# A second shared PSUM bank, and the side work laid out anew, in a windowed-attention and expert-mixing block

## The chip, the cores and the metric

The kernel runs on one core of one Trainium2 chip. The metric is the device time in microseconds of one execution.

## What is computed

The input is `x`, 16 images of 56 x 56 positions with 32 channels. Two residual blocks follow each other:

```
x = x + attention(norm(x))     # windows of 7x7 rolled by 3, 4 heads of 8 channels, mask and relative bias after the softmax
t = t + experts(norm(t))       # router over 8 experts, softmax, best 2, their outputs mixed by renormalised probability
```

In the attention the softmax comes first, and bias and mask are added to its result; so the product of bias and mask with the values is a term of its own (`ob`). The normalisations take mean and variance over the 32 channels of a position. Everything is float32 at the borders.

## The kernel before

The work is cut into 16 units (`UNITS`) of 16 x 49 positions each, a half of two images. A unit passes through these steps; `w` in a name below means an older unit, `v` a younger one.

- **Norm 1**: `load` (SP, 12 DMAs, L504), then `norm1_center` (DVE sum L852, POOL subtraction L546), `norm1_square` (ACT L683), `norm1_scale` (DVE sum L858, POOL `pow` L557 and multiplication L561). `keep` (POOL, L569) copies the input with the bias of the projection into `x_kept`, which the residual L915 of the unit two earlier reads.
- **Pre work**: `xt` 0, 1 (transposes L1128), `qk` 0 to 3 (products L1136), `place` (POOL L603) and `kmask` (ACT L723) which lay queries and keys out by head, `v` 0, 1 (L1147), `ob` 0, 1 (L1163).
- **Attention** in four groups `g`: `maximum` (PE L1181, then on DVE the reduction L874 and the two small steps L888 and L890 that write `ms`), `shift` (PE transposes L1189, ACT copy L768 to `mr`), `scores` (PE L1204 and L1210, ACT exponential L777), `pv` (PE L1225, DVE L897 and L901, POOL L611).
- **After it**: `ot` 0, 1 (PE L1236, ACT L756), `y` 0, 1 (PE L1246) with the residual `back` 0, 1 (DVE L915), norm 2 (`norm2_center`: DVE L864 and POOL L579; `norm2_square`: ACT L692; `norm2_scale`: DVE L870, POOL `pow` L590 and multiplication L594), `x2t` 0, 1 (PE L1261, ACT L786), `router` (PE L1269, DVE L922), `replicate` (7 DMAs on SP), `top2` 0 to 4 on DVE, 5 to 7 on POOL (L628 to L644), `top2_exp` (ACT).
- **Mixing**: `wt` (PE L1282, ACT L794), `mix` 0 to 16 (PE L1293 into `ps_weight`, DVE multiplication L989; at 5, 9, 13 and 16 also products L1310 into the sum in `ps_acc`, at 5 and 13 begun by L1305), `mix_drain` 0, 1 (ACT L801), `final` 0, 1 (PE L1253, DVE L998), `store` (12 DMAs).

**Order.** All engines walk one list (`program`). After a head written out in `PROLOGUE`, a `macro_step` takes one unit (`att`) through its four groups and puts side tasks between the fixed steps:

```python
for g in range(GROUPS):
    yield "scores", att, g
    yield from side((g, 0))
    ...  # "maximum" of the next group
    yield from side((g, 1))
    yield "pv", att, g
    yield from side((g, 2))
    ...  # "shift" of the next group
    yield from side((g, 3))
```

`SIDE_TASKS[(g, place)]` is written out by hand. A task is done for another unit than `att`: pre work for the next one, norm 1 for the one after that, `y` to `top2` for the one before, and `wt`, `mix` and `final` for the one before that. Each engine takes the steps of this list that are its own, strictly in order, and waits on semaphores. After the last macro step, `TAIL` names in which order the three chains that are left run: chain 0 is the mixing of unit 14, chain 1 is `ot` 1 to `top2` of unit 15, chain 2 the mixing of unit 15. Before the `wt` of unit 15, `keep_awake` issues 24 matmuls (L1093).

**Banks.** PSUM has four banks `ps_win` for the windows, `ps_pv`, `ps_weight` for the mixing's weights, `ps_acc` for its sum, and `ps_shared`, through which all 17 other fills of a unit pass one after the other (10 of the pre work, 2 `ot`, 2 `y`, 2 `x2t`, 1 `router`). `shared_free` lets PE wait, before each fill, until the fill before it in `SHARED_ORDER` has been drained.

Of the kernel before, what the change touches and what calls it, by code (L numbers as in the profile page):

```python
# [37 lines left out]
N = WS * WS  # L38
E = 8
# [30 lines left out]
PRE_ORDER = ("keep", "xt", "qk", "place", "kmask", "v", "ob")  # L70
LATE = ("wt", "mix", "mix_drain", "final", "store")
SIDE_TASKS = {
    (0, 0): [("ot", 1), ("keep", 0), ("wt", 0), ("y", 0), ("mix", 0), ("back", 0), ("mix", 1), ("y", 1), ("back", 1), ("norm2_center", 0)],
    (0, 1): [("xt", 0), ("mix", 2)],
    (0, 2): [],
    (0, 3): [("mix", 3), ("norm2_square", 0), ("xt", 1), ("mix", 4), ("norm2_scale", 0)],
    (1, 0): [("qk", 0), ("load", 0), ("mix", 5)],
    (1, 1): [("qk", 1), ("mix", 6)],
    (1, 2): [],
    (1, 3): [("mix", 7), ("qk", 2)],  # L80
    (2, 0): [("mix", 8), ("x2t", 0), ("norm1_center", 0), ("mix", 9)],
    (2, 1): [("x2t", 1), ("mix_drain", 0)],
    (2, 2): [("replicate", 0), ("kmask", 0), ("mix", 10), ("router", 0), ("mix", 11), ("qk", 3), ("place", 0), ("mix", 12), ("place", 1)],
# [5 lines left out]
}  # L89
# [10 lines left out]

TAIL = ((1, 1), (0, 1), (1, 6), (0, 1), (1, 1), (0, 11), (1, 2), (0, 1), (1, 1), (0, 1), (1, 1), (0, 1), (1, 3), (0, 1), (1, 1), (0, 2), (1, 2), (0, 4), (2, 2), (1, 1), (2, 5), (1, 1), (2, 5), (1, 1), (2, 12))


def later(name, i):

    return 1 if name in PRE_ORDER else 0 if (name, i) == ("ot", 0) else -1

# [169 lines left out]
def metaformer_block(nc, x, weights, rel_table, consts, consts_bf16, out):  # L279
    with ExitStack() as ctx:  # L280
# [192 lines left out]

        rel_list = list(rel_loads())

        def pre_bank(v, fill):

            return ps_weight if v.number == 0 and fill % 2 else ps_shared

        def weight_bank(w, fill):  # L480

# [6 lines left out]

        def token_bank(w, fill):

            spare = w.number == UNITS - 1 and fill in (1, 3)
            return ps_win[:, 3, :] if spare else ps_shared

        block = ctx.enter_context(nc.Block())

# [178 lines left out]
        def _(act):  # L674
# [172 lines left out]
        def _(dve):  # L847
# [72 lines left out]
            def router(w, _):  # L920
                dve.wait_ge(token_filled, upto("token_filled", w, 4))
                nc.vector.tensor_tensor(  # L922
                    logits[:, :, :], ps_shared[0:ROWS, 0:TOK * E].rearrange("p (t e) -> p t e", e=E),
                    rb[:, :].unsqueeze(1).to_broadcast([ROWS, TOK, E]), ALU.add).then_inc(token_drained, 1)

            at = [0]
# [160 lines left out]
        def _(pe):  # L1087
# [7 lines left out]
            def shared_free(name, u, i):  # L1095

                at = SHARED_ORDER.index((name, i))
                for back in range(1, 2 * len(SHARED_ORDER)):
                    lap, k = divmod(at - back, len(SHARED_ORDER))
                    before, j = SHARED_ORDER[k]  # L1100
                    w = u.moved(lap - later(name, i) + later(before, j))
                    if w is not None:
                        kind, first = SHARED_BANK[before]
                        drained = {"pre": pre_drained, "ot": ot_drained, "token": token_drained}[kind]
                        pe.wait_ge(drained, upto(f"{kind}_drained", w, first + j))
                        return

            def token_free(name, w, i):

                if token_bank(w, (0 if name == "y" else 2) + i) is ps_shared:  # L1110
                    shared_free(name, w, i)
                else:
                    pe.wait_ge(probs_ready, upto("probs_ready", w))

            def pre_free(v, i, fill):

# [170 lines left out]
            def mix(w, i):  # L1287
# [90 lines left out]
```

## Time and profile before

| what | value |
|---|---|
| median of 3 runs | 817.04 us (816.79 to 819.18) |
| the profiled execution | 821.02 us, its span 819.2 us |
| PE busy | 677.5 us, 83% of the span |
| DVE, POOL, ACT busy | 544.2, 516.6, 387.3 us |
| mean granted TensorE clock | 0.940 |

The span is the time from the first to the last instruction. The granted clock is 1.0 at 2.4 GHz and 0.5 at 1.2 GHz; a value between is a mean over a stretch with both.

### The profile page before, as it was taken

How to read it: one execution, taken by the hardware profiler on the slowest of the kernel's cores; microseconds unless marked ns; L12 is line 12 of the kernel's file. 1: busy time of each engine (PE TensorE's matmuls, PEld its weight loads, DVE VectorE, ACT ScalarE, POOL GpSimd, SP SyncE). 2: the span in 40 equal slices, each digit the busy share in tenths (PEclk: the TensorE clock that was granted, in tenths of full speed). 3: DMA queues.
4: the chain of work that ended last, by engine and by line, in shares of the span. 5: the costliest groups of instructions: out<-in, count | busy, mean ns of one | idle time of the engine just before them, and what ended most of it. 6: DMA issues, size and time to landing. Idle time of an engine off the chain costs nothing.

```text
span 819.2 us, 29441 instructions
## 1 busy us (share of the span) xinstructions
PE 677.5 (83%) x12632; PEld 443.1 (54%) x12632; DVE 544.2 (66%) x1003; ACT 387.3 (47%) x641; POOL 516.6 (63%) x555
## 2 busy tenths in 40 slices
PE   0777877979798989989798989989897989878675
PEld 0455554656556655645656565656556556645331
DVE  7352557867676767758676767768686667676544
ACT  1645462646464564636454554646464455612100
POOL 4736677586867768584868767685857666551520
PEclk9999898999999999979999999999998999987777
DMA  2000030313122130413131130413131030403040
GB/s 71 20 22 3 25 77 22 81 42 81 32 62 51 38 85 23 91 32 80 33 70 42 42 82 22 97 26 81 42 82 41 22 81 10 93 2 80 20 99 20
DMA packets 16961, 41.48 MB, mean 51 GB/s; under 512 B 9280, under 2 KB 9408, under 8 KB 15296
## 3 DMA queue, kind: packets, MB, share of 16 engines
q1 hardware_dynamic: 16240, 38.59, 21.2%
q8 instruction: 100, 1.64, 0.8%
q10 hardware_dynamic: 592, 1.01, 0.4%
q14 instruction: 29, 0.24, 0.1%
HBM read 7.47 MB, written 6.42 MB: 17 GB/s over the span
## 4 chain that ended last, share of the span: by engine, by line
PE 56%; DVE 23%; issue 11%; ACT 5%; POOL 4%; ACTq 0%; DVEq 0%; POOLq 0%
DVE mx L874 8%; PE ps_win L1210 7%; PE ps_acc L1310 6%; PE ps_shared L1136 6%; PE ps_weight L1293 5%; PE ps_win L1181 5%; PE ps_pv L1225 5%; PE ps_shared L1163 5%; PE ps_shared L1246 4%; DVE zt L989 4%; PE ps_shared L1147 3%; PE ps_win L1204 3%; DVE x L915 2%; DVE ms L888 2%; PE ps_acc L1305 2%
## 5 line engine op out<-in xcount | busy, mean ns | idle before, releaser
L874 DVE TENSOR_REDUCE mx<-ps_win 128x32 f32<-128x1568 f32 x64 | 114.5, 1789 | 66.5 <-PE ps_win L1181 65.9
L989 DVE TENSOR_TENSOR zt<-ps_weight,x 128x392 f32<-128x392 f32 x118 | 66.2, 561 | 83.0 <-PE ps_weight L1293 82.4
L1225 PEld LDWEIGHTS ps_pv<-vb,pt 128*49 128x49 f32 x4096 | 103.4, 127 | 14.5 <-issue 12.1
L777 ACT ACTIVATE pt<-ps_win 128x1568 f32<-128x1568 f32 x64 | 94.6, 1478 | 33.0 <-PE ps_win L1210 32.5
L611 POOL TENSOR_TENSOR on<-on,obs 128x256 f32<-128x256 f32 x64 | 46.6, 728 | 98.2 <-DVE on L901 72.6
L1225 PE MATMUL ps_pv<-vb,pt 128*49 128x18 f32 x4096 | 108.3, 200 | 0.0
L1293 PE MATMUL ps_weight<-wt,const_bf_tile 96*128 96x392 bf16 x234 | 82.3, 352 | 28.0 <-DVE zt L989 19.5
L989 DVE TENSOR_TENSOR x<-ps_weight,x 128x392 f32<-128x392 f32 x116 | 65.5, 564 | 33.3 <-PE ps_weight L1293 32.3
L768 ACT COPY mr<-ps_win 128x512 bf16<-128x512 bf16 x64 | 37.4, 584 | 87.7 <-PE ps_win L1189 87.7
L590 POOL TENSOR_TENSOR st<-st,minus_half 112x28 f32<-112x28 f32 x16 | 77.0, 4812 | 1.3
L557 POOL TENSOR_TENSOR st<-st,minus_half 112x28 f32<-112x28 f32 x16 | 76.9, 4809 | 1.3
L603 POOL TENSOR_SCALAR qbd<-qp,const_tile 128x392 f32<-128x392 f32 x128 | 76.2, 608 | 0.0
L1210 PE MATMUL ps_win<-qbd,kp 32*49 32x196 f32 x2048 | 74.7, 351 | 0.0
L723 ACT ACTIVATE kbd<-kp,const_tile 128x392 f32<-128x392 f32 x128 | 69.4, 621 | 0.0
L1181 PE MATMUL ps_win<-kbd,qp 32*49 32x196 f32 x2048 | 60.3, 344 | 6.0 <-ACT pt L777 5.1
L1136 PE MATMUL ps_shared<-xt,weight_tile 128*128 128x392 f32 x124 | 60.8, 574 | 2.1 <-ACT xt L701 0.6
L1293 PEld LDWEIGHTS ps_weight<-wt,const_bf_tile 96*128 96x128 bf16 x234 | 23.0, 98 | 71.0 <-DVE zt L989 40.6
L701 ACT COPY xt<-ps_shared 128x448 f32<-128x448 f32 (+1 forms) x31 | 15.8, 511 | 85.2 <-PE ps_shared L1128 85.2
L1181 PEld LDWEIGHTS ps_win<-kbd,qp 32*49 32x49 f32 x2048 | 35.3, 122 | 33.7 <-ACT pt L777 19.7
L1246 PE MATMUL ps_shared<-weight_tile,ot 128*112 128x128 f32 x218 | 32.7, 291 | 21.7 <-ACT ot L756 17.3
L716 ACT ACTIVATE kp<-ps_shared,weight_tile 128x392 f32<-128x392 f32 x30 | 17.6, 588 | 59.8 <-PE ps_shared L1136 59.8
L1163 PE MATMUL ps_shared<-vb,bt 128*64 128x256 f32 (+3 forms) x564 | 39.6, 280 | 6.7 <-ACT ot L756 3.0
(141 smaller groups left out, 1369.1 us busy)
## 6 DMA issues: line engine op xcount, KB each, us to landing
x<-x SPq DMA_DIRECT2D x48, 392.0 KB, 5.1
x<-x2t SPq DMA_DIRECT2D x64, 98.0 KB, 2.2
xin<-x SPq DMA_DIRECT2D x32, 150.0 KB
out<-xo SPq DMA_DIRECT2D x32, 150.0 KB
xin<-x SPq DMA_DIRECT2D x32, 18.0 KB
out<-xo SPq DMA_DIRECT2D x30, 18.0 KB
xin<-x SPq DMA_DIRECT2D x32, 15.6 KB
xin<-x SPq DMA_DIRECT2D x32, 1.9 KB
```

The lines of the kernel that those rows point to most:

```text
L557: nc.gpsimd.tensor_tensor(st1[:, 4, :], st1[:, 3, :], minus_half[:, :], ALU.pow).then_inc(rstd1, 1)
L590: nc.gpsimd.tensor_tensor(st2[:, 4, :], st2[:, 3, :], minus_half[:, :], ALU.pow).then_inc(rstd2, 1)
L603: nc.gpsimd.tensor_scalar(qbd[i][:, :, h, :], qp[v.par][:, 8 * i:8 * i + 8, :], head_rows[:, h:h + 1], 1.0, ALU.mult, ALU.mult).then_inc(q ...
L777: nc.scalar.activation(pt[g % 2].rearrange("p a x h n -> p a (x h n)"), ps_win[:, :, 0:2 * HN], ACT.Exp).then_inc(probs_ready, 1)
L874: nc.vector.tensor_reduce(mx[g % 2].rearrange("n a x h -> n a (x h)"), ps_win[:, :, 0:8 * N].rearrange("n a (k m) -> n a k m", m=N), AX, A ...
L989: nc.vector.tensor_tensor(tokens if eh else zt[:, a, :], weight_bank(w, 1 + i)[:, 0:HALF], tokens, ALU.mult).then_inc(weight_drained, 1)
L1136: mm(pre_bank(v, 2 + i)[:, 0:HALF], (wk if i % 2 else wq)[:, :], xt[:, 8 * b:8 * b + 8, :, :].rearrange("p q k i -> p (q k i)"), start=Tru ...
L1163: ins = mm(bank[PAD * x:PAD * x + PAD, groups, a0:a1, k, :], bt[:, h, last_row + column, :], values[:, x, groups, a0:a1, h, 0:2 * D], star ...
L1181: ins = mm(ps_win[PAD * k:PAD * k + N, a, HN * x:HN * x + HN], qp[u.par][r, q, :], kbd[g // 2][r, q % 8, :, :].rearrange("p h n -> p (h n) ...
L1210: ins = mm(ps_win[PAD * k:PAD * k + N, a, HN * x:HN * x + HN], kp[u.par][r, q, :], qbd[g // 2][r, q % 8, :, :].rearrange("p h n -> p (h n) ...
L1225: ins = mm(ps_pv[PAD * x:PAD * x + N, c0:c0 + SLOT], pt[g % 2][:, a, x, h, :], vb[u.par][:, 2 * g + x, a, h, :], start=True, stop=True)
L1293: mm(weight_bank(w, 1 + i)[:, 0:HALF], weight_sel[:, eh, a, :], wt[:, HALF * half:HALF * half + HALF], start=True, stop=True).then_inc(wei ...
```

## The change

`ps_acc` is used for 8 of the 17 fills as well (`ON_ACC`), in the time between its two sums of a unit. `BANK_ORDER` holds the fills and the two sums in list order, and `bank_free` waits for the last fill or sum before it in the same bank. For the first unit's pre work and for the last unit the banks are given out differently, and `tail_banks_free` waits there. The copies and the router's addition read the bank that their fill went to. `SIDE_TASKS`, `PROLOGUE` and `TAIL` are written anew; no instruction of the computation is added or removed.

```diff
-    (0, 0): [("ot", 1), ("keep", 0), ("wt", 0), ("y", 0), ("mix", 0), ("back", 0), ("mix", 1), ("y", 1), ("back", 1), ("norm2_center", 0)],
-    (0, 1): [("xt", 0), ("mix", 2)],
+    (0, 0): [("ot", 1), ("keep", 0), ("wt", 0), ("load", 0), ("y", 0), ("mix", 0), ("back", 0), ("mix", 1), ("y", 1), ("back", 1), ("norm2_center", 0), ("xt", 0), ("mix", 2)],
+    (0, 1): [("xt", 1), ("mix", 3)],
     (0, 2): [],
-    (0, 3): [("mix", 3), ("norm2_square", 0), ("xt", 1), ("mix", 4), ("norm2_scale", 0)],
-    (1, 0): [("qk", 0), ("load", 0), ("mix", 5)],
-    (1, 1): [("qk", 1), ("mix", 6)],
+    (0, 3): [("norm2_square", 0), ("qk", 0), ("mix", 4)],
+    (1, 0): [("mix", 5), ("norm2_scale", 0), ("norm1_center", 0), ("qk", 1), ("mix", 6), ("kmask", 0)],
+    (1, 1): [("mix", 7), ("qk", 2)],
     (1, 2): [],
-    (1, 3): [("mix", 7), ("qk", 2)],
-    (2, 0): [("mix", 8), ("x2t", 0), ("norm1_center", 0), ("mix", 9)],
-    (2, 1): [("x2t", 1), ("mix_drain", 0)],
-    (2, 2): [("replicate", 0), ("kmask", 0), ("mix", 10), ("router", 0), ("mix", 11), ("qk", 3), ("place", 0), ("mix", 12), ("place", 1)],
-    (2, 3): [("top2", 0), ("mix", 13), ("kmask", 1), ("top2", 1), ("v", 0), ("top2", 2)],
-    (3, 0): [("top2_exp", 0), ("mix", 14), ("top2", 3), ("v", 1), ("mix", 15), ("top2", 4)],
-    (3, 1): [("top2", 5), ("mix", 16), ("ob", 0), ("mix_drain", 1)],
-    (3, 2): [],
-    (3, 3): [("norm1_square", 0), ("final", 0), ("top2", 6), ("top2", 7), ("ot", 0), ("final", 1), ("ob", 1), ("store", 0), ("norm1_scale", 0)],
+    (1, 3): [("mix", 8)],
+    (2, 0): [("mix", 9), ("mix_drain", 0), ("mix", 10), ("place", 0), ("x2t", 0), ("mix", 11)],
+    (2, 1): [],
+    (2, 2): [("norm1_square", 0), ("qk", 3), ("x2t", 1), ("mix", 12)],
+    (2, 3): [("norm1_scale", 0), ("router", 0), ("top2", 0), ("kmask", 1)],
+    (3, 0): [("mix", 13), ("top2", 1), ("mix", 14), ("replicate", 0), ("top2", 2), ("v", 0), ("mix", 15), ("top2_exp", 0)],
+    (3, 1): [("v", 1), ("top2", 3), ("place", 1), ("mix", 16)],
+    (3, 2): [("top2", 4), ("mix_drain", 1), ("ob", 0), ("final", 0), ("top2", 5)],
+    (3, 3): [("ot", 0), ("final", 1), ("top2", 6), ("store", 0), ("top2", 7), ("ob", 1)],
...
+SUM_STARTS = {5: 0, 13: 1}
+ON_ACC = {("ot", 1), ("xt", 1), ("qk", 0), ("y", 1), ("ot", 0), ("ob", 0), ("router", 0), ("x2t", 1)}
...
+TAIL = ((1, 4), (0, 1), (1, 2), (0, 2), (1, 1), (0, 3), (1, 1), (0, 11), (1, 2), (0, 1), (1, 2), (0, 1), (1, 2),
+        (0, 2), (1, 3), (0, 2), (2, 1), (1, 1), (2, 4), (1, 1), (2, 12), (1, 1), (2, 4), (1, 1), (2, 3))
...
+            def bank_free(name, u, i):
+
+                at = BANK_ORDER.index((name, i))
+                for back in range(1, 2 * len(BANK_ORDER)):
+                    lap, k = divmod(at - back, len(BANK_ORDER))
+                    other, j = BANK_ORDER[k]
+                    if on_acc(other, j) != on_acc(name, i):
+                        continue
+                    w = u.moved(lap - later(name, i) + later(other, j))
+                    if w is None:
+                        continue
+                    if other == "sum":
+                        pe.wait_ge(sum_drained, upto("sum_drained", w, j))
+                        return
...
+            def tail_banks_free():
+
+                pe.wait_ge(ot_drained, upto("ot_drained", fixed(UNITS - 1), 0))
+                pe.wait_ge(token_drained, upto("token_drained", fixed(UNITS - 2)))
...
                 if eh == 0:
-
+                    if w.number >= UNITS - 2:
+                        tail_banks_free()
+                    else:
+                        bank_free("sum", w, half)
```

In the head, `PROLOGUE` now has the first unit's `maximum` 0 ahead of both `v`, `kmask` 0 right after `qk` 1, `kmask` 1 last, and `norm1_square` of unit 1 ahead of both `v`.

## Rows read from the trace of the kernel before

**Rows 1.** The page's head.
```profile
span 819.2 us, 29441 instructions
```

**Rows 2.** Busy time by window, one window per unit: length, engines, PEclk, DMA, GB/s.
```profile
122.16:170.91 48.75, 42.05 (x800) 27.82 (x800) 34.47 (x60) 24.05 (x41) 31.14 (x35) 0.93 0.23 51
...
304.27:349.14 44.87, 39.71 (x800) 26.75 (x800) 32.54 (x60) 24.04 (x41) 32.35 (x35) 1.00 0.26 57
349.14:398.04 48.90, 43.53 (x776) 28.26 (x776) 33.99 (x60) 24.05 (x41) 32.01 (x35) 0.90 0.23 52
...
671.10:715.79 44.69, 39.63 (x800) 26.75 (x800) 30.65 (x58) 23.30 (x40) 28.49 (x30) 1.00 0.23 51
```

**Rows 3.** Waits of PE between 120 and 740 us: total, times, longest.
```profile
PE ps_shared L1246 <- ACT ot L756: 15.9, 14, 1.2
...
PE ps_shared L1128 <- POOL xc L561: 9.4, 10, 1.0
...
PE ps_shared L1246 <- DVE x L915: 3.6, 14, 0.3
```

**Rows 4.** Timeline of PE: start, duration, instruction, idle before.
```profile
358.93 0.60 PE L1189 MATMUL ps_win<-const_bf_tile,ms 128*128 128x128 bf16 x4 [1.42 <-DVE ms L890]
...
400.83 0.91 PE L1246 MATMUL ps_shared<-weight_tile,ot 128*112 128x128 f32 x6 [0.25 <-DVE x L915]
...
403.61 0.57 PE L1128 MATMUL ps_shared<-const_tile,xc 112*128 112x112 f32 x4 [1.03 <-POOL xc L561]
...
406.02 0.40 PE L1189 MATMUL ps_win<-const_bf_tile,ms 128*128 128x128 bf16 x4
...
407.88 0.29 PE L1204 MATMUL ps_win<-mr,const_bf_tile 32*49 32x196 bf16 x8
...
429.02 0.29 PE L1204 MATMUL ps_win<-mr,const_bf_tile 32*49 32x196 bf16 x8
...
791.50 7.41 PE L1093 MATMUL ps_win<-const_bf_tile 128*128 128x512 bf16 x24 [0.67 <-DVE xo L998]
798.75 0.51 PE L1282 MATMUL ps_weight<-const_bf_tile,w_parts 112*96 112x112 bf16 x7
```

**Rows 5.** Timeline of DVE.
```profile
28.85 1.09 DVE L852 TENSOR_REDUCE st<-xin 112x28 f32<-112x896 f32 x1 [4.61 <-DMA xin<-x]
...
353.59 0.56 DVE L915 TENSOR_TENSOR x<-ps_shared,x_kept 112x384 f32<-112x384 f32 x1 [1.24 <-PE ps_shared L1246]
...
357.00 1.54 DVE L888 TENSOR_SCALAR ms<-mx 128x32 bf16<-128x32 f32 x1
...
401.78 0.56 DVE L915 TENSOR_TENSOR x<-ps_shared,x_kept 112x384 f32<-112x384 f32 x1 [0.53 <-PE ps_shared L1246]
...
405.19 0.44 DVE L888 TENSOR_SCALAR ms<-mx 128x32 bf16<-128x32 f32 x1
...
414.23 0.24 DVE L888 TENSOR_SCALAR ms<-mx 128x32 bf16<-128x32 f32 x1
...
781.06 0.39 DVE L922 TENSOR_TENSOR logits<-ps_shared,weight_tile 112x224 f32<-112x224 f32 x1 [1.09 <-PE ps_shared L1269]
...
790.90 0.55 DVE L998 TENSOR_TENSOR xo<-ps_weight,x 112x384 f32<-112x384 f32 x1
```

**Rows 6.** Timeline of POOL.
```profile
21.04 2.12 POOL L569 TENSOR_TENSOR x_kept<-xin,weight_tile 112x896 f32<-112x896 f32 x1
...
356.70 1.74 POOL L579 TENSOR_TENSOR xc<-x,st 112x896 f32<-112x896 f32 x1
...
403.42 2.11 POOL L569 TENSOR_TENSOR x_kept<-xin,weight_tile 112x896 f32<-112x896 f32 x1
...
405.81 1.74 POOL L579 TENSOR_TENSOR xc<-x,st 112x896 f32<-112x896 f32 x1
...
410.44 4.81 POOL L590 TENSOR_TENSOR st<-st,minus_half 112x28 f32<-112x28 f32 x1
...
792.65 0.61 POOL L644 TENSOR_TENSOR w_parts<-mix_rest,w_parts 112x224 bf16<-112x224 f32 x1
```

More of the change, by code:

```diff
@@ L91 @@
+    (2, 0): [("mix", 9), ("mix_drain", 0), ("mix", 10), ("place", 0), ("x2t", 0), ("mix", 11)],
[7 rows of a table added]
+}
+PRE_NAMES = (("xt", 0), ("xt", 1), ("qk", 0), ("qk", 1), ("qk", 2), ("qk", 3), ("v", 0), ("v", 1), ("ob", 0), ("ob", 1))
+TOKEN_NAMES = (("y", 0), ("y", 1), ("x2t", 0), ("x2t", 1), ("router", 0))
 SHARED_BANK = {"xt": ("pre", 0), "qk": ("pre", 2), "v": ("pre", 6), "ob": ("pre", 8), "ot": ("ot", 0),
                "y": ("token", 0), "x2t": ("token", 2), "router": ("token", 4)}
-SHARED_ORDER = [task for place in sorted(SIDE_TASKS) for task in SIDE_TASKS[place] if task[0] in SHARED_BANK]
@@ L97, with bank_order @@
-PROLOGUE = (
[4 rows of a table removed]
-TAIL = ((1, 1), (0, 1), (1, 6), (0, 1), (1, 1), (0, 11), (1, 2), (0, 1), (1, 1), (0, 1), (1, 1), (0, 1), (1, 3), (0, 1), (1, 1), (0, 2), (1, 2), (0, 4), (2, 2), (1, 1), (2, 5), (1, 1), (2, 5), (1, 1), (2, 12))
+SUM_STARTS = {5: 0, 13: 1}
+ON_ACC = {("ot", 1), ("xt", 1), ("qk", 0), ("y", 1), ("ot", 0), ("ob", 0), ("router", 0), ("x2t", 1)}
+def bank_order():
+    for place in sorted(SIDE_TASKS):
+        for name, i in SIDE_TASKS[place]:
+            if name in SHARED_BANK:
+                yield name, i
+            elif name == "mix" and i in SUM_STARTS:
+                yield "sum", SUM_STARTS[i]
@@ L474, in metaformer_block, with shared_bank, ot_bank @@
         rel_list = list(rel_loads())
+        def shared_bank(name, i):
+            return ps_acc if on_acc(name, i) else ps_shared
+        def ot_bank(u, i):
+            return ps_shared if u.number == UNITS - 1 and i else shared_bank("ot", i)
         def pre_bank(v, fill):
-            return ps_weight if v.number == 0 and fill % 2 else ps_shared
+            if v.number == 0:
+                return ps_weight if fill % 2 else ps_shared
+            return shared_bank(*PRE_NAMES[fill])
         def weight_bank(w, fill):
@@ L489, in token_bank @@
         def token_bank(w, fill):
-            spare = w.number == UNITS - 1 and fill in (1, 3)
-            return ps_win[:, 3, :] if spare else ps_shared
+            if w.number == UNITS - 1:
+                return ps_win[:, 3, :] if fill in (1, 3) else ps_shared
+            return shared_bank(*TOKEN_NAMES[fill])
         block = ctx.enter_context(nc.Block())
@@ L1093, in keep_awake @@
                     mm(ps_win[:, 0, :], identb, const_bf16_tile[:, 0:512], start=True, stop=True)
[L1095 to L1104, printed above, removed]
+            def bank_free(name, u, i):
[11 more added lines that the diff above has]
+                        return
+                    kind, first = SHARED_BANK[other]
+                    drained = {"pre": pre_drained, "ot": ot_drained, "token": token_drained}[kind]
+                    if kind == "pre" and w.number == 0:
+                        pe.wait_ge(pre_drained, upto("pre_drained", w))
+                    else:
@@ L1112, in token_free @@
                 else:
-                    pe.wait_ge(probs_ready, upto("probs_ready", w))
+                    pe.wait_ge(token_drained, upto("token_drained", w, 3 if name == "router" else 1))
             def pre_free(v, i, fill):
@@ L1298, in mix @@
                 if eh == 0:
+                    if w.number >= UNITS - 2:
+                        tail_banks_free()
+                    else:
+                        bank_free("sum", w, half)
                     if half:
```

32 lines of the change are left out of this document (21 added, 11 removed), and 8 rows, old and new, of the table PROLOGUE.

## The prediction, made before the changed kernel was run

> **What bounds the kernel now.** The page gives the span [rows 1]; the profiled execution took 821.0 us, 1.8 around its span, and lies 4.0 over the median 817.04. The second view is the busy time cut at each `wt` copy, which makes one window of each unit [rows 2]. From 122.16 to 715.79 stand 13 windows, 593.6 us, 45.66 each. PE works 39.7 of 44.87 us in a regular one: it is nearly the bound, but 5.2 us stand idle. Three windows are of another kind (48.75, 48.90 and 48.91 us, clock 0.90 to 0.93); the other ten average 44.71, so each long one costs 4.14 more.
>
> Who PE waits for is the third view [rows 3], and the timeline shows where [rows 4]. Three things matter. `y` waits for the copy of `ot` (15.9 us in all); that is data. `y` 1 waits for the residual that empties the shared bank: 0.25 a unit, 3.6 in all. `xt` 0 waits 1.03 for POOL's `norm1_scale`. So the shared bank itself is a small wait; most of what the new bank could save comes from letting tasks stand elsewhere. Also, a stop costs some 0.1 us more than its idle time, as the group before it then runs to its end.
>
> **The hidden clock.** The long windows explain themselves when DVE and POOL are laid side by side [rows 5, 6]. `ms` (L888) takes 0.24 us at 414.23. At 357.00 it takes 1.54 and ends at 358.54, just behind POOL's subtraction 356.70 to 358.44. At 405.19 it takes 0.44 and ends just behind `keep`, and the subtraction starts only at 405.81: it slips in between. It therefore matters where `keep` starts. In a regular unit POOL is late (it has just ended `norm1_scale`), `keep` starts at 403.42, and `shift` 1 starts 3.68 after the end of residual 1 (402.34 to 406.02). In the long unit POOL is free when residual 1 ends (354.15), `keep` and subtraction follow at once, and `shift` 1 comes 4.78 behind it, at 358.93 [rows 4, 5], where it lasts 0.60 instead of 0.40: PE is then at the lower clock.
>
> The Trainium skill ("SBUF — State Buffer", Who interferes with whom) says that a GpSimd instruction holds the port pair it shares with VectorE whole, and a VectorE instruction of the two-port kind waits for its end. The rows at 357.00 agree; the one at 414.23 does not, for it ran its 0.24 us under the `pow` 410.44 to 415.25 [rows 5, 6]. By the rule `ms` 2 would wait to the end of the `pow` in the new order too, 2.2 us a unit and 28 in all; by the row it waits for nothing.
>
> **Part by part.** I follow one macro step of the new list, with the times of the unit at 398 as a base.
>
> *`y` 1 on `ps_acc`.* It no longer waits for residual 0: 0.25 and the 0.1 of the stop. Residual 1 ends near 401.92 instead of 402.34.
>
> *`norm1_scale` from the end of the step to (2, 3).* The 1.03 in front of `xt` 0 goes: its input is ready about 10 us earlier. But `keep` now finds POOL free, starts at 401.95 and is followed by the subtraction, so that every unit is placed like the long ones: `shift` 1 at 401.92 + 4.7 = 406.6 instead of 406.02. Both `xt` now stand before `pv` 0, and `mix` 3 waits 0.4 us. From `shift` 1, `qk` 0 (0.75) and `mix` 4 (0.2) follow, so `scores` 1 comes at 407.8 instead of 407.88 [rows 4], with `qk` 0 already done.
>
> *Group 1.* DVE has both sums (1.0 each) before `mix` 6 and the reduction of group 2. The exponential, `maximum`, reduction and `shift` then set the pace and `scores` 2 comes at 416.1, as before, with one `mix` more done. The 0.75 in hand is lost there as idle time (0.6 before `scores` 2).
>
> *`load` in (0, 0), `norm1_center` in (1, 0).* The sum needs the input. In the head the load began when `keep` ended at 23.16, and the sum started on its arrival at 28.85: 5.7 us [rows 5, 6]. Here `keep` ends at 404.1, the input is there at 409.8, and DVE wants it at 410.8. Hidden, by 1 us; without this cover the reduction behind it is late by as much.
>
> *Group 2.* `router` and `qk` 3 each take a bank and the 0.44 wait of the old `mix` 13 goes; `router` waits 0.3 for the copy of `x2t` 1, since ACT's `norm1_square` and the copy of `qk` 3 are ahead. `place` 0 now runs when `ms` 3 wants to start, which costs up to one of its four 0.6 us pieces. `scores` 3 comes at 425.2. Before, it came at 429.02 [rows 4] with 2.9 us more done (`mix` 13, its four-part start and products, `v` 0). Ahead by 0.9.
>
> *Group 3.* `v` 1 waits 0.3 for the copy of `v` 0, which is behind the exponential and in the same bank. `final` 1 waits 0.25 instead of 0.44, although `top2` 4 now stands before `final` 0 on DVE. `top2` 5 to 7 on POOL end 0.2 to 0.3 us before `y` 0 would be held up by `wt`. Ahead by 1.0.
>
> Such a walk misses small stops, so I take 0.9 a unit: 13 x 0.9 = 11.7 us.
>
> *Clock falls.* Idle between 397 and 407 us is 3.3 us in the new order (1.13, 0.66, 0.4, 1.1) against 3.6 before (1.13, 0.66, 0.25, 1.03, 0.57), so falls should be no more frequent; and one costs less, 3.0 instead of 4.14, since the later `shift` 1 (1.1) is paid already. I take two in the new kernel. The profiled execution had three, and the median, 4.0 lower, about two. From two to two: 2 x (4.14 - 3.0) = 2.3 us saved.
>
> *Tail.* `wt` of unit 15 starts at 798.75, but POOL has ended `top2` at 793.26: it waits for `keep_awake`, 7.25 us of matmuls that begin when `final` 1 of unit 14 is added (791.45) [rows 4 to 6]. Both `final` stood behind all of `top2` 0 to 4 on DVE; now `final` 0 is after `top2` 1 and `final` 1 ahead of `top2` 4, as the multiplications ran in POOL's 7 us of norm 2. `y` 0 is also before `wt` of unit 14: 0.65. From the router's addition (781.06, now 780.4): 2.5 for `top2` 0 and 1, up to 0.4 of waiting, 0.6 for `final` 0, 2.4 for `top2` 2 and 3, 0.55 plus latencies for `final` 1: 787.1. That is 4.4 us earlier, and all behind it moves along: POOL ends at 792.9, `keep_awake` at 794.3. Bounds: 0 if the mixing is late and `final` with it; 5.8 if POOL becomes the bound.
>
> *Head.* `kmask` 1 behind both `ob` puts 2.2 us before the first exponential, and `xt` 0 of unit 1 now stands before `maximum` 1 and waits for POOL until about 42; that is 2 us lost. In group 3 of that step `v` 0 is behind `scores` 3 instead of before it and `norm1_scale` is earlier, 2 to 3 us won. Zero, from -2 to +2. The last macro step, which waits on the chain at a low clock, zero, within 1.
>
> Sum: 11.7 + 2.3 + 4.4 = 18.4, from the median: **799 us**. From the profiled execution, with one fall more: 22.5 from 821.0, the same.
>
> **Rivals.**
> - *No fall* (0.17): the denser stretch keeps the clock. The two falls' 6 us more: 793; with the head's 2, the tail's 1.4 and 0.1 a unit more, 788.
> - *The side work makes new waits* (0.17). POOL's chain `norm1_scale`, `place` 1, `pv`, `top2` 5 to 7 has 0.3 us to spare; or DVE's `top2` 2, which ends 0.4 us before POOL's 1.7 us multiplication L561 starts, runs into it. One us a unit: 799 + 13 = 812. The Trainium skill (same page and section) speaks for it: a VectorE instruction with two SBUF inputs also waits for a GpSimd one that reads SBUF.
> - *Only the order differs* (0.07): PE's work is the same, the waits come back elsewhere, and only the tail is felt in part: 815 to 819.
> - *The clock falls in every unit* (0.11), at `shift` 1, which now comes as late behind residual 1 as in the three long units. 11 falls more at 3.0: 832. Break-even at about nine falls of 13. Against it: in the long unit at 349 PE was slow already before `shift` 1, for its wait there was only 1.42.
> - My forecast has 0.48, from 795 to 806.
>
> No change that can be told from none lies within 0.3%, 2.5 us. Faster is 0.48 + 0.17 + 0.17 and most of nothing else: 0.82; same 0.07; slower 0.11. The range 788 to 813 leaves out the last two.
>
> **What would show it.** Windows from `wt` copy to `wt` copy of 43.5 to 44 us; no wait of L1128 for POOL and none of `y` 1 for the residual; `keep` right behind each residual 1 and `ms` 1 of 0.9 to 1 us; `shift` 1 4.7 us behind residual 1; `final` 1 of unit 14 ahead of `top2` 4, and `wt` of unit 15 some 13.9 us behind the start of its router's addition instead of 17.7. Wrong if DVE waits for the input in (1, 0), if `wt` waits for POOL, or if more than four windows show a clock under 1.

## The result, and the profile after

The changed kernel takes 808.35 us (median of four runs, 804.47 to 821.45) beside 817.12 for the kernel before: ratio 0.9875, 95% interval 0.9831 to 0.9919. That is 1.2% less time, clear of no change; it lies inside the predicted range, but 9.4 us above the predicted 799. Measured again later it took 802.61 (six runs, ratio 0.9837, 0.9804 to 0.9871). The median of all ten is 804.3. Medians here are of all runs, while a ratio leaves out the runs that lie over 1.5% above the fastest of their kernel (here the 821.45).

The profiled execution of the changed kernel took 804.47 us, 1.8 of them around its span. The page's head answers to [rows 1]:

```profile
span 802.7 us, 29444 instructions
```

So the two profiled executions differ by 16.5 us. The busy time by window, cut at the `wt` copies (columns as in [rows 2]), shows a pair of regular units and one in which the clock fell:

```profile
344.09:388.30 44.21, 38.76 (x774) 25.86 (x776) 33.76 (x60) 24.70 (x42) 32.15 (x34) 1.00 0.26 57
388.30:432.30 44.00, 39.17 (x798) 26.56 (x800) 33.73 (x60) 24.57 (x41) 32.15 (x34) 1.00 0.24 54
432.30:479.37 47.07, 41.23 (x774) 26.70 (x776) 33.73 (x60) 24.67 (x41) 32.01 (x34) 0.93 0.25 57
```

Of the kernel before, the same view shows that its regular units are of two kinds, which alternate:

```profile
398.04:442.92 44.88, 39.71 (x800) 26.75 (x800) 32.54 (x60) 24.05 (x42) 32.36 (x35) 1.00 0.24 53
442.92:487.15 44.23, 39.28 (x776) 26.16 (x776) 32.35 (x60) 24.03 (x41) 31.94 (x35) 1.00 0.27 60
```

They differ in the work of `ob` (24 instructions and 0.43 us less on PE in the shorter kind). Cut at the `wt` copies, the kind of 44.88 seems to have become 44.00 and that of 44.23 to have stayed at 44.21. But after the change `wt` waits for POOL, and that moves the cut. Cut at `y` 0, which stands near the start of every macro step (two units before the change, then two after it):

```profile
398.31 1.10 PE L1246 MATMUL ps_shared<-weight_tile,ot 128*112 128x128 f32 x8 [1.13 <-ACT ot L756]
443.18 1.10 PE L1246 MATMUL ps_shared<-weight_tile,ot 128*112 128x128 f32 x8 [1.13 <-ACT ot L756]
487.42 1.10 PE L1246 MATMUL ps_shared<-weight_tile,ot 128*112 128x128 f32 x8 [1.13 <-ACT ot L756]
```

```profile
344.36 1.10 PE L1300 MATMUL ps_shared<-weight_tile,ot 128*112 128x128 f32 x8 [0.54 <-ACT ot L789]
388.36 1.10 PE L1300 MATMUL ps_shared<-weight_tile,ot 128*112 128x128 f32 x8
432.57 1.10 PE L1300 MATMUL ps_shared<-weight_tile,ot 128*112 128x128 f32 x8 [0.32 <-ACT ot L789]
```

the longer kind goes from 44.87 (398.31 to 443.18) to 44.21 (388.36 to 432.57), the shorter from 44.24 to 44.00. A pair of units is 0.90 shorter by either cut, 0.45 a unit. The waits of PE between 120 and 740 us answer to [rows 3] (in all, times, longest):

```profile
PE ps_weight L1348 <- DVE zt L1022: 19.2, 41, 1.0
PE ps_win L1240 <- DVE ms L923: 18.5, 25, 1.5
PE ps_weight L1337 <- POOL w_parts L677: 12.1, 14, 2.8
PE ps_shared L1198 <- ACT vb L768: 6.1, 12, 0.5
```

`xt` no longer waits for POOL and `y` 1 no longer for the residual. In their place `shift` (L1240) waits for `ms` in every regular unit, `v` 1 (L1198) for `vb`, and `wt` (L1337) for POOL. The last is 0.64 to 0.86 us in twelve of its 14 times (0.42 and 2.76 in the others), and there it stands in time that `y` 0 spent waiting for `ot` before. The timeline of PE (behind `y` 0 at 388.36), then DVE, then POOL in the unit at 388, which answers to the unit at 398 in [rows 4 to 6]:

```profile
396.67 0.40 PE L1240 MATMUL ps_win<-const_bf_tile,ms 128*128 128x128 bf16 x4 [1.22 <-DVE ms L923]
...
415.49 0.29 PE L1255 MATMUL ps_win<-mr,const_bf_tile 32*49 32x196 bf16 x8
...
421.38 1.08 PE L1198 MATMUL ps_shared<-weight_tile,xt 128*49 128x128 f32 x16 [0.51 <-ACT vb L768]
```

```profile
391.33 0.56 DVE L948 TENSOR_TENSOR x<-ps_acc,x_kept 112x384 f32<-112x384 f32 x1
...
395.21 1.07 DVE L921 TENSOR_SCALAR ms<-mx 128x32 bf16<-128x32 f32 x1
...
404.43 0.24 DVE L921 TENSOR_SCALAR ms<-mx 128x32 bf16<-128x32 f32 x1
...
412.43 0.47 DVE L921 TENSOR_SCALAR ms<-mx 128x32 bf16<-128x32 f32 x1
```

```profile
392.05 2.11 POOL L602 TENSOR_TENSOR x_kept<-xin,weight_tile 112x896 f32<-112x896 f32 x1 [4.45 <-DVE x L948]
...
394.44 1.74 POOL L612 TENSOR_TENSOR xc<-x,st 112x896 f32<-112x896 f32 x1
...
401.65 4.80 POOL L623 TENSOR_TENSOR st<-st,minus_half 112x28 f32<-112x28 f32 x1
...
411.08 2.30 POOL L636 TENSOR_SCALAR qbd<-qp,const_tile 128x392 f32<-128x392 f32 x4
```

`keep` (L602) starts 0.16 behind the end of residual 1 and is followed by the subtraction (L612). `ms` 1, 0.24 us long when nothing holds it (404.43, under the `pow`), takes 1.07 at 395.21, to just behind the subtraction's end at 396.18, and `shift` 1 comes 4.78 behind the residual. The tail, PE and POOL:

```profile
776.11 7.74 PE L1126 MATMUL ps_win<-const_bf_tile 128*128 128x512 bf16 x23 [3.40 <-DVE xo L1031]
783.68 0.51 PE L1337 MATMUL ps_weight<-const_bf_tile,w_parts 112*96 112x112 bf16 x7
```

```profile
780.54 0.61 POOL L677 TENSOR_TENSOR w_parts<-mix_rest,w_parts 112x224 bf16<-112x224 f32 x1
```

The 16.5 us, stretch by stretch (means over the windows at clock 1.00: 44.61 before, 44.21 after):

| stretch | before | after | saved |
|---|---|---|---|
| head, to the first window | 122.16 | 121.78 | 0.4 |
| 13 windows, 13 x the regular length | 579.9 | 574.7 | 5.2 |
| 13 windows, the rest (falls of the clock) | 13.7 | 8.9 | 4.8 |
| last macro step | 46.98 | 45.70 | 1.3 |
| tail | 56.43 | 51.64 | 4.8 |

### The profile page after: what moved, and what is told of

It is laid out like the page before. It is cut to its first block, busy times and chain, and to the rows that moved or that the text cites. A ratio compares the mean times of both kernels' runs of the same rounds, so it can differ in the third digit from the quotient of the medians.

```text
span 802.7 us, 29444 instructions
## 1 busy us (share of the span) xinstructions
PE 665.8 (83%) x12602; PEld 439.5 (55%) x12632; DVE 553.3 (69%) x1003; ACT 395.0 (49%) x641; POOL 515.8 (64%) x555
## 4 chain that ended last, share of the span: by engine, by line
PE 43%; DVE 36%; issue 8%; POOL 7%; ACT 4%; SPq 0%; DMA 0%; DVEq 0%; POOLq 0%; ACTq 0%
DVE mx L907 9%; PE ps_win L1261 5%; PE ps_weight L1348 4%; PE ps_pv L1276 4%; PE ps_acc L1368 4%; PE ps_win L1232 4%; DVE ms L921 4%; DVE zt L1022 3%; PE ps_shared L1187 3%; DVE x L1022 3%; PE ps_shared L1300 2%; PE ps_win L1255 2%; PE ps_win L1240 2%; DVE ms L923 2%; PE ps_acc L1187 2%
## 5 line engine op out<-in xcount | busy, mean ns | idle before, releaser
L1276 PEld LDWEIGHTS ps_pv<-vb,pt 128*49 128x49 f32 x4096 | 101.2, 128 | 25.6 <-issue 25.3
L602 POOL TENSOR_TENSOR x_kept<-xin,weight_tile 112x896 f32<-112x896 f32 x16 | 33.9, 2120 | 68.6 <-DVE x L948 68.6
L768 ACT COPY vb<-ps_shared 49x512 f32<-49x512 f32 x62 | 36.8, 593 | 40.5 <-PE ps_shared L1198 40.2
L1187 PE MATMUL ps_shared<-xt,weight_tile 128*128 128x392 f32 x94 | 44.1, 552 | 0.6 <-ACT xt L734 0.6
L1240 PE MATMUL ps_win<-const_bf_tile,ms 128*128 128x128 bf16 x256 | 26.5, 229 | 21.8 <-DVE ms L923 21.2
L1255 PE MATMUL ps_win<-mr,const_bf_tile 32*49 32x196 bf16 x1024 | 37.1, 267 | 7.2 <-ACT mr L801 7.2
```

The costliest lines, as they stand in the source:

```text
L1187: mm(pre_bank(v, 2 + i)[:, 0:HALF], (wk if i % 2 else wq)[:, :], xt[:, 8 * b:8 * b + 8, :, :].rearrange("p q k i -> p (q k i)"), start=Tru ...
L1276: ins = mm(ps_pv[PAD * x:PAD * x + N, c0:c0 + SLOT], pt[g % 2][:, a, x, h, :], vb[u.par][:, 2 * g + x, a, h, :], start=True, stop=True)
```

## The experiments

Every kernel was timed in five rounds beside the kernel before, which took 817.2 to 818.4 us. A window is the time between two `wt` copies. The granted clock named with a run is the mean of its execution.

**The changed kernel once more (e0_after_again).**

> The changed kernel again, to see its spread. Its four runs lie at 804.5, 804.8, 811.9 and 821.5 us. Theory A (the spread is the number of units in which TensorE's clock falls): time and mean granted clock go together, about 0.7 us for each 0.001 of clock. Rival B (something else varies, DMA or the start): times differ at equal clock.

It took 802.61 us. Its runs and those of the first measurement line up by the clock: 0.959 took 796.75, 0.957 799.32, 0.946 804.47, 0.936 811.91 and 0.921 821.45. At nearly equal clocks they still differ, by up to 4 us (0.945 took 808.48, 0.944 took 804.79). Its profiled execution, the one of 796.75, has 11 windows between 43.90 and 44.77, one of 45.15 and one of 45.21. Most of the spread of the changed kernel is the clock.

**The new layout with one bank (e1_layout_one_bank).**

```
-ON_ACC = {("ot", 1), ("xt", 1), ("qk", 0), ("y", 1), ("ot", 0), ("ob", 0), ("router", 0), ("x2t", 1)}
+ON_ACC = set()
```

> The changed kernel with ON_ACC empty: its lists, but all 17 fills in ps_shared. Theory A (the second bank is what lets the tasks stand where they do): y 1 waits for residual 0 again (0.35 us), xt 0 for residual 1 ahead of maximum 1 (1.0), x2t 1 for the copy of qk 3 (0.7): some 2 us a unit, so 26 us over the changed kernel, about 835. Rival B (the lists alone give the gain, the bank is idle decoration): within 3 us of the changed kernel's 808.

834.34 us, ratio 1.0154 (1.0101 to 1.0207). At clock 1.00 its windows are 1.4 longer than those of the changed kernel:

```profile
359.99:405.58 45.59, 39.10 (x774) 25.77 (x776) 33.88 (x60) 24.77 (x42) 32.10 (x34) 1.00 0.24 55
405.58:450.97 45.39, 39.50 (x798) 26.49 (x800) 33.89 (x60) 24.64 (x41) 32.11 (x34) 1.00 0.23 53
```

The bank's waits are back: `x2t` for the copy of `kp` (0.7 in each unit), `xt` 0 and `y` 1 for the residual (0.7 and 0.3). The new order needs the second bank. 13 x 1.4 are 18 of the 30 us over the changed kernel's 804.3; the rest goes with a lower clock (its runs have 0.906 to 0.948, the changed kernel's 0.921 to 0.959).

**The second bank with the old order (e2_bank_alone, then e10_bank_alone_fewer).** `SIDE_TASKS`, `PROLOGUE` and `TAIL` are those of the kernel before. In e2 six fills go to `ps_acc`, in e10 three:

```
-ON_ACC = {("ot", 1), ("xt", 1), ("qk", 0), ("y", 1), ("ot", 0), ("router", 0)}
+ON_ACC = {("ot", 1), ("y", 1), ("ot", 0)}
```

> The old PROLOGUE, SIDE_TASKS and TAIL, with six of the fills (ot 0, ot 1, y 1, xt 1, qk 0, router) in ps_acc; x2t 1 and ob 0 stay in ps_shared, because in the old list they stand ahead of the copy of the sum. Theory A: only the waits on the bank go, 0.35 us a unit at y 1, and the wait of xt 0 for POOL stays: 812 to 816. Rival B (the bank alone is the gain): about 808.

> The lists of before with only ot 1, y 1 and ot 0 in the summing bank (e2_bank_alone had xt 1, qk 0 and the router there too). Theory A, e2 lost its time because the start of the mixing's sum now stands behind qk 0 in this bank, whose copy comes behind an exponential on ScalarE (1.1 us in each unit), and by the falls of the clock that this wait brings: without it windows at full clock are those of before or 0.3 less (44.2 to 44.6), and the time is 812 to 819. Rival B, in these lists any use of the second bank shifts the chain of the first norm (its waits of xt 0 for POOL grew from 1.0 to 1.5 us): over 825.

850.86 us (1.0426, 1.0402 to 1.045) and 839.73 us (1.0236, 1.0186 to 1.0287). For e2 no theory had this; for e10 it is what rival B said, and by the wait that it named. In e2 the start of the mixing's sum waits up to 1.1 (0.8 on average) for the copy of `qk` 0, and even at full clock a unit takes 2.8 us more than before:

```profile
458.38:505.41 47.03, 38.71 (x774) 26.04 (x776) 34.94 (x60) 24.13 (x41) 31.96 (x35) 1.00 0.25 56
```

In e10 that wait is gone and the time still is 22 us over the kernel before. What both have is a wait of `xt` 0 for POOL's `norm1_scale` of 1.5 and 1.6 on average, longer than the 1.03 of [rows 4]: `y` 1 comes earlier and POOL's chain does not. The waits of PE in e10:

```profile
PE ps_shared L1178 <- POOL xc L593: 21.0, 13, 3.0
```

In none of its 13 windows does the clock stay at 1.00 (the profiled execution, 854.4 us, is the longest of its six, whose mean clocks are 0.886 to 0.920). A window with such a fall, and four-microsecond cuts of it (PE is the first engine, PEclk the column behind the fifth):

```profile
262.13:313.68 51.55, 45.80 (x776) 29.30 (x776) 34.26 (x60) 24.03 (x41) 31.97 (x35) 0.83 0.22 51
```

```profile
264.00:268.00 4.00, 2.18 (x43) 1.71 (x44) 3.94 (x6) 0.00 (x0) 3.92 (x3) 1.00 0.01 1
268.00:272.00 4.00, 4.00 (x76) 3.46 (x74) 3.45 (x7) 1.22 (x3) 3.82 (x4) 0.61 0.18 52
272.00:276.00 4.00, 3.90 (x54) 1.92 (x53) 1.81 (x3) 2.39 (x3) 1.80 (x4) 0.54 0.20 57
```

PE was idle for 1.8 of the 4 us before 268, and then stood at the lower level, 1.2 GHz, for most of 7 us.

**The same with the wait filled (e12_fill_before_xt).** e10 with products that nobody reads, in front of `xt` 0's wait for POOL, in the bank that it fills next:

```
 pre_free(v, i, i)
+if i == 0 and v.number != 0:
+    for _ in range(6):
+        mm(pre_bank(v, 0)[:, :], identb, const_bf16_tile[:, 0:512], start=True, stop=True)
 pe.wait_ge(normed1, upto("normed1", v))
```

> The kernel of e10_bank_alone_fewer with 6 matrix products of no use (128x512, bf16, into the bank that xt 0 is to fill) between the wait of xt 0 for its bank and its wait for POOL's scaling, so in the wait of 1.6 us there. Nothing else is taken away. Theory A, it is TensorE's idle time in this wait that lets the clock fall in nearly every unit of e10 (no window there is at 1.00): with it filled the clock goes from 0.90 to 0.94 or more, regular windows come to 44.8 to 45.5 at 1.00, and the time falls by 15 us or more, to 812 to 825. Rival B, the falls come from something else in these lists (many waits together, or the length of the unit): clock under 0.92 and the time within 5 us of 840, or above for what the fillers push.

817.04 us, 22.7 less than e10, by work alone that has no use; the ratio is 0.9845 (0.9815 to 0.9875), and the three quickest of its seven runs take 803.9 to 806.5 at a clock of 0.960 to 0.962, where e10's six have 830.8 to 854.4 at 0.886 to 0.920. Nine of 13 windows stand at 1.00, where e10 has none:

```profile
357.60:401.84 44.24, 39.74 (x779) 26.71 (x782) 33.02 (x60) 24.05 (x42) 31.93 (x35) 1.00 0.24 55
401.84:446.71 44.87, 40.17 (x803) 27.30 (x806) 33.20 (x60) 24.04 (x41) 32.34 (x35) 1.00 0.26 60
```

Two things follow. The idle time in front of `xt` 0 is what lets the clock fall in most units of e10; in e12's first four windows (48.75, 50.99, 51.65 and 45.20 us) it falls all the same. And once it does not fall, the old order with the second bank runs at 44.24 and 44.87, the two lengths of the kernel before: without new places for the tasks the bank shortens no unit. What the same six products would do in the kernel before, whose `xt` 0 waits 1.03, was not run; since e12's quickest runs are as quick as the changed kernel's median, that other way to the same time stands open.

**The old tail (e3_old_tail).** The changed kernel with `TAIL` of before.

> The changed kernel with the old merging of the last three chains (TAIL) and nothing else. Theory A, the tail is a term of its own: the stretch from the last regular copy of wt to the end grows back by the 4.8 us that the traces show between the two kernels (51.6 to 56.4), everything before it stays, so 4 to 5 us more than the changed kernel at the same clock. Rival B, the old merging was only late in the old order of the units, and the sparing of the tail came with the shorter units: under 1.5 us more.

808.01 us. From the last `wt` copy but one to the end its profiled execution takes 55.9 where the changed kernel's takes 51.6, though the macro step ahead of it is 1.4 shorter there. The changed kernel's second profiled execution has 51.3. The median is 3.7 over the 804.3 of the ten runs, but the intervals of the ratios overlap (0.9818 to 0.9903 here), so it is the traces that show the tail as a term of its own, of about 4 us; the medians agree with it.

**A shorter keep_awake (e6_keep_awake_16).** `range(24)` becomes `range(16)`.

> The changed kernel with 16 instead of 24 matrix products of no use in front of the last turning of wt. They held it 2.5 us past the last step of POOL. Theory A: they end 2.5 us earlier (8 x 0.32), wt is turned right behind POOL's last step, and the end comes 2.2 to 2.5 us earlier at the same clock. Rival B, the clock is low in what follows because TensorE then stands idle: the stretch behind wt grows by 1 us or more, and the time is the same to 1 us less.

808.81 us. In its profiled execution `wt` follows POOL's last step (its end is at 801.83) at once, where in the changed kernel it came 2.5 us behind:

```profile
801.89 0.55 PE L1337 MATMUL ps_weight<-const_bf_tile,w_parts 112*96 112x112 bf16 x7 [0.29 <-POOL w_parts L677]
```

So the hold is gone, as theory A said. The window between the last two `wt` copies is 2.45 shorter than in the changed kernel's first profiled execution (30.72 after 33.17), but that proves nothing: in its second, with all 24 products, the same window is 30.65, at a clock of 0.72 and not 0.69 (e0's row, then e6's).

```profile
743.72:774.37 30.65, 23.06 (x112) 9.56 (x113) 16.66 (x36) 3.83 (x8) 13.25 (x13) 0.72 0.31 66
771.75:802.47 30.72, 23.29 (x105) 10.24 (x105) 16.67 (x36) 3.93 (x7) 13.27 (x13) 0.66 0.31 66
```

At a clock of 0.935 to 0.939 the runs take 808.6 to 810.0, and the changed kernel took 811.9 at 0.936, but the median is not lower. A gain of this size is below what six runs of this spread tell.

**Fillers before each shift (e5_fill_before_shift).** Ahead of L1240:

```
+pe.wait_ge(max_taken, upto("max_taken", u, g))
+for _ in range(4 if g == 1 else 2):
+    mm(ps_win[:, 1, :], identb, const_bf16_tile[:, 0:512], start=True, stop=True)
 pe.wait_ge(shift_split, upto("shift_split", u, g))
```

> The changed kernel with matrix products of no use (128x512, bf16, into a bank that nobody reads then) in front of each turning of the shift, 4 before the first group's successor and 2 before the others: they stand in the wait of 1.2 us for ms and in the short ones. Theory A, the clock falls because TensorE stands idle in just these waits: the clock of the profile goes to 0.97 or more, windows of 45 us and over vanish but for the first, runs spread less, median 797 to 801 at a regular unit of at most 44.4. Rival B, what the clock follows lies elsewhere (the long waits in front of the products of the mixing, or nothing that the order sets): same clock (0.92 to 0.96), same spread, and the time the same or 1 to 3 us more for what the fillers push.

807.8 us: neither theory whole. The falls do vanish. All windows but the first (50.13, 0.84) and the fourth (0.96) are at 1.00, and the six runs lie within 7.7 us where the changed kernel's ten lie within 24.7 (the six of e0 within 11.7):

```profile
356.50:401.04 44.54, 40.89 (x786) 26.73 (x786) 33.73 (x60) 24.61 (x42) 32.21 (x34) 1.00 0.26 60
401.04:445.37 44.33, 41.26 (x810) 27.44 (x810) 33.73 (x60) 24.48 (x41) 32.22 (x34) 1.00 0.26 57
```

But a regular unit costs 0.33 more, 4.3 in all, and at a clock of 0.955 to 0.962 the runs take 802.9 to 809.4, where the changed kernel took 796.8 and 799.3 at 0.959 and 0.957. What is won through the clock is paid back. The first window differs between the profiled executions of the changed order without fillers too (44.91, in e6 48.65), so its length here shows nothing of the fillers.

**keep behind `pv` 0 (e4_keep_after_pv0).** So that `ms` 1 is not held. The load waits for `keep`, so the norm's start moves too:

```
-(0, 0): [("ot", 1), ("keep", 0), ("wt", 0), ("load", 0), ("y", 0), ...
+(0, 0): [("ot", 1), ("wt", 0), ("y", 0), ...
-(0, 2): [],
+(0, 2): [("keep", 0), ("load", 0)],
```

and `norm1_center` goes from (1, 0) to (2, 0), behind `mix` 10.

> The changed kernel with keep and load moved from (0, 0) to (0, 2), so that on POOL the subtraction of norm 2 comes straight after residual 1 and is over before ms 1 wants to start, and norm1_center moved to (2, 0) for its input. Theory A (POOL's subtraction holds ms 1 up, and this wait is on the path): ms 1 takes 0.24 instead of 1.08 us, shift 1 comes about 0.8 us earlier, the idle time before it falls from 1.22 to about 0.4; 0.4 to 0.8 us a unit, so 5 to 10 us under the changed kernel, and with fewer falls of the clock a narrower spread, about 798. Rival B (the chain of group 1 takes it back): shift 1 earlier, but the same time, 805 to 808.

815.76 us (0.9979, 0.9953 to 1.0005). The first half came as expected: `ms` 1 takes 0.24, `shift` 1 stands 0.39 idle instead of 1.22. The second did not. With the first norm late, POOL's L594 runs when `top2` 2 is on DVE (the timelines of POOL, DVE and PE):

```profile
339.08 1.70 POOL L594 TENSOR_TENSOR xc<-xc,st 112x896 f32<-112x896 f32 x1
```

```profile
339.21 1.74 DVE L996 TENSOR_TENSOR top<-top 112x28 f32<-112x28 f32 x1
```

```profile
341.61 0.87 PE L1368 MATMUL ps_acc<-x,weight_tile 128*32 128x392 f32 x8 [0.72 <-DVE x L1022]
```

L996, 0.19 us otherwise, takes 1.74 and the products behind it wait. The windows are 44.6 and 44.8, and the time is above what either theory had. The shorter wait in front of `shift` 1 did not bring fewer falls of the clock: five of the 13 windows are under 1.00, and in four of them PE goes to the lower clock right at that `shift` 1 or in the product behind it, after 0.39 us of waiting.

**The center earlier again (e7_keep_center_apart).** As e4, but `norm1_center` in (1, 1), behind `mix` 7, and `norm2_scale` ahead of `mix` 5.

> keep and the load behind pv 0, as in the run before that moved them, but the first norm's sum and centering only one place later (behind the maximum of group 2) and the second norm's scaling ahead of the mixing's product 5. Theory A, it is where POOL's additions stand that costs, and the earlier try lost its gain only by the late centering: ms of group 1 takes 0.24 us, shift 1 comes 0.8 us earlier, POOL's scaling of the second norm starts 1 us earlier, and the unit keeps 0.6 to 0.8 of it: regular windows 43.4 to 43.7, 8 to 10 us less in all at the same clock. Rival B, what is won at shift 1 is lost again at the next fixed point (top2 on VectorE under POOL's scaling, the waits for x2t or vb): windows 44.1 to 44.5 and no difference.

850.43 us (1.0345, 1.0296 to 1.0393), worse than anything forecast. DVE, in order, now reaches the sum before its input (timeline of DVE, then PE, then the cut by windows):

```profile
341.67 1.09 DVE L885 TENSOR_REDUCE st<-xin 112x28 f32<-112x896 f32 x1 [1.17 <-DMA xin<-x]
```

```profile
344.01 0.34 PE L1348 MATMUL ps_weight<-wt,const_bf_tile 96*128 96x392 bf16 x1 [1.58 <-DVE zt L1022]
```

```profile
342.00:345.00 3.00, 1.42 (x25) 0.32 (x13) 2.49 (x5) 1.48 (x1) 2.92 (x4) 1.00 0.01 3
345.00:348.00 3.00, 2.72 (x42) 1.38 (x38) 1.13 (x2) 1.87 (x3) 3.00 (x6) 0.62 0.00 0
348.00:351.00 3.00, 3.00 (x73) 2.92 (x66) 2.39 (x4) 0.00 (x0) 0.08 (x1) 0.50 0.02 5
```

DVE waits 1.17 for the load, PE 1.58 for DVE, and behind these PE stays at 0.50 (1.2 GHz) until 357. Windows of this kind last 51 to 53 us, those without a fall 45.6 to 46.1 (43.05 in the last of the 13, where there is less to do).

**One place later (e8_center_behind_8).** As e7, but:

```
-(1, 1): [("mix", 7), ("norm1_center", 0), ("qk", 2)],
+(1, 1): [("mix", 7), ("qk", 2)],
-(1, 3): [("mix", 8)],
+(1, 3): [("mix", 8), ("norm1_center", 0)],
```

> The kernel of e7_keep_center_apart with the first norm's sum and centering one place later again, behind the mixing's product 8. In e7 VectorE stood 1.2 us (0.8 in the quicker units) at this sum for the load that starts behind keep, TensorE then 1.2 to 1.8 us for zt, and in five of twelve units the clock fell right there. Theory A, that wait alone made e7 slow: VectorE waits for no load between 120 and 700 us, windows at full clock take 43.3 to 43.8, the falls become no more frequent than in the changed kernel, and the time is 792 to 802. Rival B, what shift 1 wins is lost at the waits that stand behind it anyway (router for x2t, top2 against POOL's scaling): windows 44.1 to 44.8 at full clock, 800 to 812.

792.57 us, ratio 0.966 (0.9607 to 0.9712), better than both kernels. No wait for a load is left between 120 and 720 us. In the timelines of DVE and POOL, `ms` 1 is no longer under the subtraction: that runs at 340.60 for 1.75, and `keep` comes behind `ms`:

```profile
342.34 0.24 DVE L921 TENSOR_SCALAR ms<-mx 128x32 bf16<-128x32 f32 x1
```

```profile
344.81 2.13 POOL L602 TENSOR_TENSOR x_kept<-xin,weight_tile 112x896 f32<-112x896 f32 x1
```

and the regular windows are 43.25 and 43.07, 0.96 and 0.93 under those of the changed kernel, with 11 of 13 at 1.00:

```profile
335.23:378.48 43.25, 39.20 (x776) 25.84 (x776) 32.77 (x60) 24.69 (x41) 32.13 (x34) 1.00 0.26 58
378.48:421.55 43.07, 39.60 (x800) 26.55 (x800) 32.78 (x60) 24.59 (x41) 32.14 (x34) 1.00 0.25 55
```

In the one regular unit that fell (at 464, 45.77 us, 0.96) PE is at the lower clock from `shift` 1 on, which lasts 0.61 instead of 0.40 behind a wait of only 0.39, no longer than in the units beside it that did not fall:

```profile
472.34 0.61 PE L1240 MATMUL ps_win<-const_bf_tile,ms 128*128 128x128 bf16 x4 [0.39 <-DVE ms L923]
```

**Both edits (e9_best).** e8 with the shorter `keep_awake`.

> The kernel of e8_center_behind_8 with keep_awake cut from 24 to 16 matrix products, as in e6_keep_awake_16. There the profile showed the stretch from the last copy of wt but one shorter by 2.45 us. Theory A, the two edits add up: 30 to 32 us lower in ratio terms to the kernel before than none, median 788 to 792, at equal clock 2 us under e8. Rival B, the end is then set by the clock, which has fallen by the last unit: no difference from e8 (791 to 794).

796.95 us (0.9732, 0.9695 to 0.9769). Its regular windows are e8's; 790 to 810 with a clock of 0.961 to 0.926. The shorter `keep_awake` shows no gain here either. The intervals of e8 and e9 just overlap, so the two cannot be told apart; e8 has the lower median.

## Why the prediction was right, and where it was 9 us off

- **`y` 1 on `ps_acc`, `norm1_scale` moved: right.** Both waits are gone, and e1 shows that the bank carries this: without it 1.4 us a unit and 834.34 us. That the bank by itself brings little was right too, and more sharply than put: e12's regular windows are those of before, and without its fillers the bank alone costs 2.4% (e10, 1.9 to 2.9).
- **`keep` behind residual 1, `ms` 1 long, `shift` 1 at +4.7: right**, to 0.1 (0.16, 1.07, 4.78). The kernel e8 puts a price on it: `keep` elsewhere, with `norm2_scale` ahead of `mix` 5 and a cover for the load, is worth 0.9 to 1.0 in each unit. The prediction saw this cost and counted it only as 0.6 at `shift` 1.
- **"so I take 0.9 a unit: 13 x 0.9 = 11.7 us": this term was mis-sized.** It measured 5.2. Two steps of it failed. First, the walk's own unit won 0.66 and not 0.9 (`y` 0 to `y` 0, 44.87 to 44.21). Laid on the unit at 388 so that `y` 0 agrees, `shift` 1, `scores` 1 and `scores` 2 are within 0.03 of the walk, but `scores` 3 is 0.24 late (`ms` 3 held by `place` 0), `v` 1 waits 0.51 and not 0.3, and the lead at the next `scores` 0 is 0.67 and not 1.0. That the window between `wt` copies is 44.00, where 0.9 off 44.88 gives 43.98, is luck of the cut. Second, the walk's unit was of the slower kind, and it stood for all. The other kind, with 0.43 less work on PE and a wait of 0.81 at `xt` 0, won 0.24 (44.24 to 44.00). It had less to win at `xt` 0, and of its shorter `ob` it loses 0.2 at `final` 1, which waits 0.44 for DVE where the slower kind waits 0.24. [rows 2] had only windows of 44.87 and 44.69 among its regular ones; the average of 44.71 stood in the text and was not asked why it lay under 44.87.
- **Load hidden by 1 us: right** for the regular units; the wait for it that the prediction named as a way to go wrong is what made e7 45.6 at full clock, and 51 with its falls.
- **Clock falls: the place right, the number not.** Five of the 13 windows of the profiled execution are under 1.00 (0.92, 0.93, 0.96, 0.93, 0.96), where two were put and more than four were named as a sign of being wrong; in all but the first `shift` 1 lasts 0.57 to 0.61 instead of 0.40. Each of these four is smaller than thought, 1.5 to 2.9 us over its kind where 3.0 was put. In the second profiled execution only the first window is under 1.00. The break-even of the rival with falls in every unit is eight falls and not nine, by its own terms (817 less 799 is six falls of 3.0, beside the two). The excess of the long windows fell from 13.7 to 8.9 us in the profiled executions, 4.8 saved where 22.5 - 11.7 - 4.4 = 6.4 was put. The medians cannot be split so: the changed kernel's runs go from 0.921 to 0.959 in clock, and its ten take 796.75 to 821.45. A run with hardly a fall takes 797, the figure of the rival without falls was 793.
- **Tail 4.4: right** (4.8 in the traces, 3.7 in e3's median). `final` 1 of unit 14 stands ahead of `top2` 4's end, `keep_awake` holds `wt` by 2.5, and `wt` comes 14.75 behind the router's addition, 13.9 put.
- **Head 0 and last macro step 0: 0.4 and 1.3**, inside the first's bounds and 0.3 outside the second's. In all the profiled executions differ by 6.0 less than the 22.5 put: 6.5 less in the units, 1.6 less in the falls, and 2.1 more in tail, head and last step, of which 1.7 were not forecast.
- **The rivals.** "The clock falls in every unit" did not happen in this kernel, but in e10. `top2` 2 running into L594, the mechanism of the second rival, did not happen here (0.19) but in e4 (1.74). In e10 the falls come behind `xt` 0, and not at `shift` 1 as the rival had it.

What stays open: why the changed kernel's falls differ so from run to run of the same instructions, and which wait starts one. In e10 it is shown to be the idle time in front of `xt` 0. For the changed order e5 shows that the falls go when the waits in front of all four `shift` are filled; but the wait of 1.2 us (once 1.5) in front of `shift` 1 passed without a fall in all twelve units of e0 that have it, and in e4 and e8 the clock fell at the same place behind 0.39. The fall of the first window was not tested; in the two profiled executions of the changed kernel and in e5 it comes right behind a wait of `wt` for POOL of 2.8 to 3.5 us. Which of the tasks' new places gives the 0.45 a unit was not tried one by one, and neither was the head.

## What to carry to other kernels

Measure the unit of a walk against its neighbours: where two kinds alternate, walk both. And cut where nothing new waits, or the cut itself moves. When an order is changed, look at the clock of each window and not only at the waits: waits of 1.5 to 1.7 were followed by a lower clock in nearly every unit (e10), and useless products in them gave the time back; those of 1.2 went by in one execution and not in the next, and a unit could fall behind 0.39 as well, so no single length tells. And a small VectorE instruction on the critical chain belongs under a `pow` or under nothing on GpSimd, never under its large subtractions and multiplications (1.07 to 1.54 instead of 0.24, 1.74 instead of 0.19).

## What the runs showed of the hardware

Waits of PE of 1.2 to 1.8 us (in most units of e10, in some of e7) are followed by stretches of 3 to 17 us at 1.2 GHz, and the unit takes 0.6 to 7 us longer; waits of 1.2 in the changed kernel by stretches of 3 to 7 us in some units, 1.5 to 2.9 us longer. Filling the wait with six useless products made a kernel 22.7 us faster (e12). The Trainium skill ("TensorE: Matmul & The Clock Gate", Loop structure matters more than you think) gives a wait of 8 us for a DMA as its example of what makes matmuls run slow; the runs here show it for far shorter ones.

`ms` (one input) ran its 0.24 under the `pow`, took 1.07 under the subtraction L612 and 0.47 under the four pieces of `place`; L996 (two inputs in SBUF) went from 0.19 to 1.74 under L594. Of the Trainium skill's rule ("SBUF — State Buffer", Who interferes with whom) the traces agree with the part on two inputs from SBUF; its part on the whole instruction is right for L612 and L594 and not for the `pow`.
